# One fp32 matmul per sample on four column tiles for the Gram products of a recommendation network

## The chip, the cores and the metric

The kernel runs on one core of one Trainium2 chip. The metric is the device time of one execution in microseconds (us). A core has five engines that work side by side and meet at semaphores: TensorE (PE, with its weight loads shown apart as PEld), VectorE (DVE), ScalarE (ACT), GpSimd (POOL) and SyncE (SP), which here issues all DMA transfers. TensorE writes to PSUM (8 banks of 128 partitions x 512 fp32 values); everything else lives in SBUF.

## The reference

2048 samples, each a 27 x 128 matrix x. Each sample's Gram matrix x x^T gives 351 pair products (below the diagonal), which together with the sample's first row feed five dense layers (480 to 1024, 1024, 512, 256 and 1 outputs).

```python
bottom_mlp_output = bottom_output[:, 0, :]
interaction = jnp.einsum('bnd,bmd->bnm', bottom_output, bottom_output)
interaction_flat = interaction[:, _TRIL_R, _TRIL_C]
x = jnp.concatenate([bottom_mlp_output, interaction_flat, zero_pad], axis=1)
x = jax.nn.relu(x @ W0.T + b0)
x = jax.nn.relu(x @ W1.T + b1)
x = jax.nn.relu(x @ W2.T + b2)
x = jax.nn.relu(x @ W3.T + b3)
return x @ W4.T + b4
```

All is float32.

## The kernel before

**Chunks and layers.** The samples are worked on in 4 chunks of 512 (CHUNK). The dense layers hold the features in partitions and the samples in columns, and each fp32 product is split in two parts of a reduced type (fp32r): hi is the rounded value, lo the rest, and `product` (L1115) adds three matmuls, lo x hi, hi x hi and hi x lo (L1117 to L1119), in one PSUM bank. Two banks (`work`) take turns for the tiles of layers 0 and 1; four (`acc`) collect layers 2 to 4; two (`gps`) hold the Grams and the transposed pairs. The last chunk's layer 1 runs in another form (`layers_last`) that has no part in this. ScalarE applies the relu, VectorE splits its output into hi and lo.

**Slices.** The inputs come in slices of 32 samples (SLICE_GROUPS = 8 groups of GROUP = 4 samples), 16 slices a chunk: 128 partitions (the 128 values of an input row) x 864 columns (32 samples x 27 rows), 432 KB each. Four slices make a sub-chunk of 128 samples (SUB). One chunk's Grams are made while the chunk ahead of it goes through its layers; only chunk 0's stand by themselves.

**Grams of chunks 1 to 3.** For a slice, VectorE writes xs from xraw: hi (L733), then lo (L735), each sample padded to 32 columns (`input_parts`). A Gram half (`gram_half`) is 16 samples: four matmuls (L1143), each with four samples' hi as weights (123 columns) and their hi and lo as moving columns (224). Only the four diagonal blocks of the result are of use. ScalarE takes them out of PSUM with four copies, one for each block of 32 partitions (L541). VectorE adds 0.5 x (hi hi) + (hi lo) for a slice (`half_sum`, L751); after each fourth slice it transposes 32 x 32 blocks (L793) and adds each picked block to its mirrored one (L797, `pair_products`), which gives 378 pair slots. TensorE transposes them (L1156), ScalarE and VectorE write them as hi and lo into featH and featL, the input of layer 0.

**Grams of chunk 0.** VectorE copies each slice, padded, into xpad (`pad_input`, L969). Eight plain fp32 matmuls a slice (`first_gram`, L1129) take four samples as weights (128 columns) and 108 moving columns into two banks. ScalarE takes out four blocks a slice (L557), VectorE transposes and picks (`first_pairs`, L782 and L786). Then `layer0_left` computes the first 256 samples' layer 0, after which the first Gram half of chunk 1 and two tiles of the rest run. Before them VectorE clears the padding of xs (`zero_pads`, L963), for which TensorE waits (L1355, L1374).

**Order.** Each engine's order is written by hand. `plans` names the steps (one product of a dense layer each) after which a Gram half and a transposition stand: in chunks 1 to 3's making one half about every third step, with `interleave` doing the same for ScalarE and VectorE. xraw has XSLOTS = 4 slots, xfirst (chunk 0 only) 8 more. SyncE issues x, w0, w1, w2 and w3 in one queue (`load_x`, `load_w1`, `keep_w1`, `refill_w1`): a slot of xraw is filled again when its lo part is made, xs when the Grams four slices back are done.

Of the kernel before, what the change touches and what calls it, by code (L numbers as in the profile page):

```python
# [18 lines left out]
EVEN = INPUTS + INPUTS % 2  # L19
GCOLS = GROUP * EVEN  # L20
USED = (GROUP - 1) * QUAD + INPUTS
# [19 lines left out]
XSLOTS = 4  # L41
FIRST_SLOTS = 2 * XSLOTS
# [44 lines left out]
def rec_program(nc, x_t, x0_t, w0, w1, w2, w3, w4, biases, b4, out):  # L87
# [5 lines left out]
    with ctx:  # L93
# [19 lines left out]
        with nc.sbuf_tensor("xfirst", [P, FIRST_SLOTS, SCOLS], f32) as xfirst:  # L113
            pass
# [19 lines left out]
        xraw = sb("xraw", [P, XSLOTS, SCOLS])  # L134
        x0raw = sb("x0raw", [P, CHUNK])
        grams2 = sb("grams2", [P, 2, SLICE_GROUPS, 2, INPUTS])
# [10 lines left out]
        with nc.sbuf_tensor("xpad", [P, 2 * XSLOTS, SLICE_GROUPS * GROUP, QUAD], f32) as xpad:  # L147
            pass

        xs = sb("xs", [P, XSLOTS, 2, SLICE_GROUPS * GROUP, QUAD], f32r)  # L150

# [16 lines left out]
        x_first = [sem(f"x_first{i}") for i in range(XSLOTS + FIRST_SLOTS)]  # L168
# [3 lines left out]
        xpads_zero, pads_done = sem("xpads_zero"), sem("pads_done")  # L172
# [7 lines left out]
        xpad_done = sem("xpad_done")  # L180
        xh_done, xl_done = sem("xh_done"), sem("xl_done")
        gram_done, grams_out, half_sums = sem("gram_done"), sem("grams_out"), sem("half_sums")
# [24 lines left out]
        def by_sample(buf, p):  # L207
            return buf[:, p % XSLOTS, :].rearrange("p (b n) -> p b n", n=INPUTS)

        def first_slot(p):  # L210

            if XSLOTS <= p < XSLOTS + FIRST_SLOTS:
                return xfirst[:, p - XSLOTS, :]
            return xraw[:, p % XSLOTS, :]

        def loads_of_slot(g, p):

            return SLICES // XSLOTS * (g - 1) + 1 + p // XSLOTS + 1
# [40 lines left out]

        def parts(g, p):  # L260

            return SLICES * (g - 1) + p + 1
# [66 lines left out]
        AHEAD = XSLOTS - 1  # L329

        def loads_at(m):

            return range(2 * m + 2 * XSLOTS + 2, min(2 * m + 2 * XSLOTS + 4, SLICES))
# [4 lines left out]
        def first_banks(p):  # L338

            banks = gps[:, :, :], acc[:, 0:2, :], work[:, :, :]  # L340
            return banks[p % 3]

        def banks_used(p):

            return p - 3

        def first_grams(s):

            return grams2[:, :, :, :, :].rearrange("p a g t n -> p (a g t) n") if s % 2 else grams[:, :, :]
# [38 lines left out]
        def _(sp):  # L388
            def load_x(g, p):
                n = SLICES * g + p  # L390
                if n < XSLOTS + FIRST_SLOTS:
                    sp.dma_start(first_slot(p), x_t[n, :, :]).then_inc(x_first[p], 16)
                    return
                if n < SLICES:
                    sp.wait_ge(xpad_done, n - XSLOTS - FIRST_SLOTS + 1)
                elif n < SLICES + XSLOTS:
                    sp.wait_ge(xpad_done, n - XSLOTS + 1)
                elif p < XSLOTS:
                    sp.wait_ge(gram_done, 2 * (n - XSLOTS + 1))
                else:  # L400
                    sp.wait_ge(xl_done, parts(g, p - XSLOTS))
                sp.dma_start(xraw[:, p % XSLOTS, :], x_t[n, :, :]).then_inc(x_in[p % XSLOTS], 16)
# [68 lines left out]
            def body(c):  # L471
# [3 lines left out]
                if c == 0:  # L475
                    x_before_keep = {0: (4, 5), 1: (6, 7, 8), 2: (9, 10), 3: (11, 12), 4: (13, 14), 5: (15,)}
                elif more:
                    for p in range(XSLOTS, 2 * XSLOTS + 2):
                        load_x(c + 1, p)
# [49 lines left out]
        def _(act):  # L529
            def grams_from_psum(g, h):  # L530

                n = HALVES * g + h
                act.wait_ge(gram_done, n + 1)
                if h % 2 == 0 and h >= 4:
                    act.wait_ge(half_sums, SLICES * (g - 1) + h // 2 - 1)
                at = h % 2 * HALF_GROUPS
                for q in range(GROUP):
                    rows = slice(q * QUAD, min((q + 1) * QUAD, USED))
                    src = gps[rows].rearrange("p b (g w) -> p (b g) w", w=2 * P)[:, :, 0:2 * GCOLS]
                    src = src.rearrange("p g (t c) -> p g t c", c=GCOLS)  # L540
                    last = act.activation(grams2[rows, h // 2 % 2, at:at + HALF_GROUPS, :, :],  # L541
                                          src[:, :, :, q * EVEN:q * EVEN + INPUTS], ACT.Copy)
                last.then_inc(grams_out, 1)

            def first_from_psum(p):
# [6 lines left out]
                for q in range(GROUP):  # L552
                    rows = slice(q * QUAD, (q + 1) * QUAD)
                    src = first_banks(p)[rows, :, 0:HALF_GROUPS * GROUP * INPUTS]
                    src = src.rearrange("p b (g c) -> p b g c", c=GROUP * INPUTS)
                    dst = first_grams(s)[rows, at:at + SLICE_GROUPS, :].rearrange("p (b g) n -> p b g n", b=2)
                    last = act.activation(dst, src[:, :, :, q * INPUTS:(q + 1) * INPUTS], ACT.Copy)  # L557
                last.then_inc(grams_out, 2)
# [165 lines left out]
        def _(dve):  # L724
            for i in range(XSLOTS):
                dve.memset(xpad[:, 2 * i:2 * i + 2, :, INPUTS:], 0.0).then_inc(xpads_zero, 1)

            def input_parts(g, p):
                n = SLICES * g + p
                hi, lo = xs[:, p % XSLOTS, 0, :, 0:INPUTS], xs[:, p % XSLOTS, 1, :, 0:INPUTS]  # L730
                dve.wait_ge(x_in[p % XSLOTS], 16 * loads_of_slot(g, p))
                ge(dve, gram_done, 2 * (n - XSLOTS + 1))
                dve.tensor_copy(hi, by_sample(xraw, p)).then_inc(xh_done, 1)  # L733
                dve.wait_ge(xh_done, parts(g, p))
                dve.tensor_tensor(lo, by_sample(xraw, p), hi.bitcast(f32), ALU.subtract).then_inc(xl_done, 1)  # L735
# [8 lines left out]

            def half_sum(g, p):

                n = SLICES * g + p
                dve.wait_ge(grams_out, 2 * (n + 1))
                ge(dve, turned_done, SUBS * g + p // SLICES_SUB)
                at = p % SLICES_SUB * SLICE_GROUPS  # L750
                dve.scalar_tensor_tensor(out=grams[0:USED, at:at + SLICE_GROUPS, :],  # L751
                                         in0=grams2[0:USED, p % 2, :, 0, :], scalar=0.5,
                                         in1=grams2[0:USED, p % 2, :, 1, :], op0=ALU.mult, op1=ALU.add)\
                   .then_inc(half_sums, 1)

            def rectangles():
# [3 lines left out]
                def both(at, col, blocks, apart, rows, cols):  # L760
# [4 lines left out]
                    across = bass.AP(v.tensor, v.offset + col * QUAD,  # L765
                                     [v.ap[0], (apart * DIAG, blocks), (1, rows), (QUAD, cols)])
                    return dst, direct, across
# [10 lines left out]
            def first_pairs(s):  # L778

                dve.wait_ge(grams_out, 2 * SLICES_SUB * (s + 1))  # L780
                ge(dve, pairs_done, PAIR_OPS * s)
                dve.transpose(turned[:, :, :], first_grams(s).rearrange("p g m -> p m g")).then_inc(turned_done, 1)  # L782
                dve.wait_ge(turned_done, s + 1)
                ge(dve, pairs_t, s)
                for dst, one, _ in rectangles():
                    dve.tensor_copy(dst, one).then_inc(pairs_done, 1)  # L786

            def pair_products(g, s):

                n = SUBS * g + s  # L790
                dve.wait_ge(half_sums, SLICES_SUB * (n + 1 - SUBS))
                dve.wait_ge(pairs_done, PAIR_OPS * n)
                dve.transpose(turned[:, :, :], grams[:, :, :].rearrange("p g m -> p m g")).then_inc(turned_done, 1)  # L793
                dve.wait_ge(turned_done, n + 1)
                dve.wait_ge(pairs_t, n)
                for dst, one, other in rectangles():
                    dve.tensor_tensor(dst, one, other, ALU.add).then_inc(pairs_done, 1)  # L797

            def half_point(g, h):

                p = h // 2
                if h % 2 == 0:
                    ahead = AHEAD if g > 1 else AHEAD - 1
                    if p + ahead < SLICES:
                        input_parts(g, p + ahead)
                else:
                    half_sum(g, p)
                    if p % SLICES_SUB == SLICES_SUB - 1:
                        pair_products(g, p // SLICES_SUB)
# [151 lines left out]
            def zero_pads(i):  # L961
# [480 lines left out]
```

## Time and profile before

| | us |
|---|---|
| median of the runs (3) | 476.79 |
| lowest and highest | 475.68, 477.36 |
| the profiled execution | 477.05 |
| its span, first to last instruction | 475.3 |
| TensorE, VectorE, ScalarE busy in it | 464.9, 321.1, 264.6 |

The profiled execution's own time is 1.75 us over its span, which is what lies around the program. Its mean granted TensorE clock is 0.996 of full speed (1.00 is 2.4 GHz). A busy time is the sum of an engine's instructions; on TensorE, whose matmuls overlap, the distance from one start to the next is the better measure. An fp32 matmul of the program stands in the trace as two records of weight load and two of matmul, an fp32r one as one of each.

### The profile page before, as it was taken

Reading aid. Unit: us, or ns where it says so; the run is one execution under the profiler, and the core shown is the slowest. Engines: PE = TensorE matmul, PEld = TensorE weight load, DVE = VectorE, ACT = ScalarE, POOL = GpSimd, SP = SyncE. Lnnn points to the kernel's source line nnn. Section 1 sums busy time; section 2 is a strip of 40 time slices with the busy share of each in tenths; the row PEclk is TensorE's granted clock in tenths of the full one; section 3 lists DMA queues with packets and bytes.
Section 4 is the critical chain, followed back from the end, with each engine's and each line's share of the span. In section 5 each row is a group of like instructions: output and inputs, shape, how many; then the busy total and the mean of one; then the engine's idle time right before and its main releaser. Section 6 shows DMA issues by size and latency. Waiting matters only on the chain.

```text
span 475.3 us, 7112 instructions
## 1 busy us (share of the span) xinstructions
PE 464.9 (98%) x2599; PEld 397.1 (84%) x2599; DVE 321.1 (68%) x570; ACT 264.6 (56%) x615; POOL 0.7 (0%) x6
## 2 busy tenths in 40 slices
PE   8999899999999999999999999999999999999996
PEld 8998888888888788888888878888888778899983
DVE  4698679796849878574616877765725988766244
ACT  3896477677664377555563366565553556233241
POOL 0000000000000000000000000000000000000000
PEclk9999899999999999999999999999999999999999
DMA  8998626856225630743345243653234420460100
GB/s 301 383 341 292 207 76 207 299 192 226 92 90 201 263 106 23 308 164 116 131 159 210 56 132 125 238 215 125 90 94 170 137 89 0 134 214 11 44 1 0
DMA packets 24226, 74.40 MB, mean 157 GB/s; under 512 B 3072, under 2 KB 9216, under 8 KB 20608
## 3 DMA queue, kind: packets, MB, share of 16 engines
q1 hardware_dynamic: 24192, 73.95, 44.1%
q8 instruction: 21, 0.34, 0.3%
q14 instruction: 13, 0.11, 0.1%
HBM read 65.55 MB, written 8.40 MB: 156 GB/s over the span
## 4 chain that ended last, share of the span: by engine, by line
PE 87%; DVE 7%; ACT 4%; issue 2%; POOLq 0%; POOL 0%; DVEq 0%
PE work L1117 16%; PE work L1119 15%; PE work L1118 15%; PE gps L1143 9%; PE acc L1117 8%; PE acc L1119 7%; PE acc L1118 7%; ACT grams L557 2%; PE gps L1129 1%; PE gps L1119 1%; PE gps L1118 1%; PE gps L1117 1%; PE work L1129 1%; PE acc L1129 1%; ACT w0h L592 1%
## 5 line engine op out<-in xcount | busy, mean ns | idle before, releaser
L541 ACT ACTIVATE grams<-gps 32x216 f32<-32x216 f32 (+1 forms) x384 | 131.4, 342 | 86.5 <-PE gps L1143 83.0
L1117 PE MATMUL work<-h1h,w1s 128*128 128x512 f32 (+1 forms) x208 | 81.1, 390 | 0.0
L1119 PE MATMUL work<-h1l,w1s 128*128 128x512 f32 (+1 forms) x208 | 80.2, 386 | 0.0
L1118 PE MATMUL work<-h1h,w1s 128*128 128x512 f32 (+1 forms) x208 | 79.3, 381 | 0.0
L1143 PEld LDWEIGHTS gps<-xs 128*123 128x123 f32 x384 | 55.3, 186 | 9.7 <-issue 2.1
L1117 PE MATMUL work<-featH,w0l 126*128 126x512 f32 (+5 forms) x160 | 57.2, 358 | 3.3 <-DVE xs L963 2.1
L1143 PE MATMUL gps<-xs 128*123 128x224 f32 x384 | 57.7, 272 | 0.0
L1118 PE MATMUL work<-featH,w0h 126*128 126x512 f32 (+5 forms) x160 | 56.3, 352 | 0.0
L751 DVE SCALAR_TENSOR_TENSOR grams<-grams 123x216 f32<-123x216 f32 x48 | 18.4, 383 | 56.2 <-ACT grams L541 56.2
L1119 PE MATMUL work<-featL,w0h 126*128 126x512 f32 (+5 forms) x160 | 56.0, 350 | 0.0
L735 DVE TENSOR_TENSOR xs<-xraw,xs 128x864 fp32r<-128x864 f32 x48 | 50.8, 1059 | 1.7
L1117 PE MATMUL acc<-h2h,w2l 128*128 128x512 f32 x128 | 51.0, 399 | 0.3 <-DVE w2l L954 0.3
L576 ACT ACTIVATE act_out<-work,bias 128x512 f32<-128x512 f32 (+1 forms) x56 | 36.7, 658 | 25.6 <-PE work L1119 24.3
L1119 PE MATMUL acc<-h2l,w2h 128*128 128x512 f32 x128 | 50.3, 393 | 0.0
L1118 PE MATMUL acc<-h2h,w2h 128*128 128x512 f32 x128 | 49.9, 390 | 0.0
L1119 PEld LDWEIGHTS work<-h1l,w1s 128*128 128x128 f32 x208 | 39.1, 188 | 8.3
L1117 PEld LDWEIGHTS work<-h1h,w1s 128*128 128x128 f32 x208 | 39.3, 189 | 5.6 <-DVE w1s L949 0.4
L1118 PEld LDWEIGHTS work<-h1h,w1s 128*128 128x128 f32 x208 | 39.4, 190 | 5.4
L829 DVE TENSOR_TENSOR h2l<-act_out,h2h 128x512 fp32r<-128x512 f32 x40 | 27.7, 693 | 14.7 <-ACT act_out L637 13.6
L1117 PEld LDWEIGHTS work<-featH,w0l 126*128 126x128 f32 (+2 forms) x160 | 30.8, 193 | 8.0 <-DVE xs L963 2.3
L1119 PEld LDWEIGHTS work<-featL,w0h 126*128 126x128 f32 (+2 forms) x160 | 30.8, 192 | 4.0
L1118 PEld LDWEIGHTS work<-featH,w0h 126*128 126x128 f32 (+2 forms) x160 | 31.0, 194 | 3.3
(124 smaller groups left out, 699.3 us busy)
## 6 DMA issues: line engine op xcount, KB each, us to landing
xraw<-x_t SPq DMA_DIRECT2D x56, 432.0 KB, 4.7
w1s<-w_parts SPq DMA_DIRECT2D x20, 1024.0 KB, 4.8
stage<-w_t SPq DMA_DIRECT2D x16, 512.0 KB, 5.7
w_parts<-w1s SPq DMA_DIRECT2D x8, 1024.0 KB, 4.9
xfirst<-x_t SPq DMA_DIRECT2D x8, 432.0 KB, 8.5
w0raw<-w_t SPq DMA_DIRECT2D x4, 512.0 KB, 9.5
w2raw<-w_t SPq DMA_DIRECT2D x4, 512.0 KB, 6.6
h1l<-w_parts SPq DMA_DIRECT2D x8, 256.0 KB, 4.0
```

The costliest lines, as they stand in the source:

```text
L541: last = act.activation(grams2[rows, h // 2 % 2, at:at + HALF_GROUPS, :, :], src[:, :, :, q * EVEN:q * EVEN + INPUTS], ACT.Copy)
L557: last = act.activation(dst, src[:, :, :, q * INPUTS:(q + 1) * INPUTS], ACT.Copy)
L576: act.activation(act_out[:, slot(layer, m, more), cols], bank[:, cols], ACT.Relu, bias=bias[:, row:row + 1]).then_inc(relu_done, 1)
L592: act.activation(w0_piece(w0h, n), w0_piece(w0raw, n), ACT.Copy).then_inc(w0_hi, 1)
L735: dve.tensor_tensor(lo, by_sample(xraw, p), hi.bitcast(f32), ALU.subtract).then_inc(xl_done, 1)
L751: dve.scalar_tensor_tensor(out=grams[0:USED, at:at + SLICE_GROUPS, :], in0=grams2[0:USED, p % 2, :, 0, :], scalar=0.5, in1=grams2[0:USED, ...
L829: dve.tensor_tensor(lo, full, hi.bitcast(f32), ALU.subtract).then_inc(split_done, 1)
L1117: pe.matmul(dst, wl, ah, start=start, stop=False)
L1118: pe.matmul(dst, wh, ah, start=False, stop=False)
L1119: return pe.matmul(dst, wh, al, start=False, stop=stop)
L1129: last = pe.matmul(first_banks(p)[:, k // HALF_GROUPS, at:at + GROUP * INPUTS], four.rearrange("p b n -> p (b n)"), four[:, :, 0:INPUTS], ...
L1143: last = pe.matmul(gps[0:USED, j // 2, j % 2 * 2 * P:j % 2 * 2 * P + 2 * GCOLS], xs[:, p % XSLOTS, 0, four, :].rearrange("p b n -> p (b n) ...
```

## The change

All Grams, of every chunk, are made in one way: each sample by a plain fp32 matmul of its own, with the sample's 27 columns of the landed slice both as weights and as moving columns. Sample q of each four goes to column tile q (`tile_position=(0, 32 q)`), so that its 27 x 27 result lies in partitions 32 q to 32 q + 26, in columns of its own group.

- No padded or split copy of the input: `input_parts`, `pad_input`, `zero_pads`, xs and xpad are gone, and so is `half_sum`. VectorE clears six banks once at the start.
- One copy out of PSUM for a half (128 x 108) or, in chunk 0, for a slice (128 x 216), where there were four. A half now takes one bank and the halves alternate, so TensorE waits for the copy before the last one (`grams_out`, n - 1).
- `pair_picks` copies one block of each mirrored pair in all chunks, where chunks 1 to 3 added the two.
- xraw has 8 slots, xfirst 8; chunk 0's 16 slices are loaded without a wait. Later loads wait for the Gram that last read the slot, and their places in SyncE's queue are moved.
- Chunk 0 uses six banks in turn, and its transpositions, w0's hi parts and VectorE's steps stand in a new order.

```diff
-XSLOTS = 4
-FIRST_SLOTS = 2 * XSLOTS
+XSLOTS = 8
...
-        W0_HI_AFTER = [8, 10, 12, 14]
+        W0_HI_AFTER = [10, 12, 14, 15]
-        TRANSPOSE_AT = SLICES_SUB + 2
+        TRANSPOSE_AT = SLICES_SUB + 3
...
+                sp.wait_ge(gram_done, 2 * ((p if g == 1 and p < XSLOTS else n - XSLOTS) + 1))
                 sp.dma_start(xraw[:, p % XSLOTS, :], x_t[n, :, :]).then_inc(x_in[p % XSLOTS], 16)
...
-                    x_before_keep = {0: (4, 5), 1: (6, 7, 8), 2: (9, 10), 3: (11, 12), 4: (13, 14), 5: (15,)}
+                    x_before_keep = {0: (8,), 1: (9,), 2: (10, 11), 3: (12, 13), 4: (14,), 5: (15,)}
...
-                for q in range(GROUP):
-                    rows = slice(q * QUAD, min((q + 1) * QUAD, USED))
...
+                act.activation(sub_grams(sub)[:, at:at + HALF_GROUPS, :],
+                               gps[:, h % 2, 0:HALF_COLS].rearrange("p (g n) -> p g n", n=INPUTS), ACT.Copy)\
+                   .then_inc(grams_out, 1)
...
+            def grams_of(bank, samples, groups):
+
+                for j, k in enumerate(groups):
+                    for q in range(GROUP):
+                        one = samples[:, (k * GROUP + q) * INPUTS:(k * GROUP + q + 1) * INPUTS]
+                        last = pe.matmul(bank[q * QUAD:q * QUAD + INPUTS, j * INPUTS:(j + 1) * INPUTS], one, one,
+                                         start=True, stop=True, tile_position=(0, q * QUAD))
+                return last
...
             def gram_half(g, h, turned_before):
 
                 n, p = HALVES * g + h, h // 2
-                pe.wait_ge(xl_done, parts(g, p))
-                pe.wait_ge(grams_out, n)
+                if h % 2 == 0:
+                    pe.wait_ge(x_in[p % XSLOTS], 16 * loads_of_slot(g, p))
+                pe.wait_ge(grams_out, n - 1)
                 if g > 1 or turned_before:
                     pe.wait_ge(pairs_lo, SUBS * g + turned_before)
-                for j in range(HALF_GROUPS):
-                    k = h % 2 * HALF_GROUPS + j
-                    four = slice(k * GROUP, (k + 1) * GROUP)
-                    last = pe.matmul(gps[0:USED, j // 2, j % 2 * 2 * P:j % 2 * 2 * P + 2 * GCOLS],
-                                     xs[:, p % XSLOTS, 0, four, :].rearrange("p b n -> p (b n)")[:, 0:USED],
-                                     xs[:, p % XSLOTS, :, four, 0:EVEN], start=True, stop=True)
-                last.then_inc(gram_done, 1)
+                groups = range(h % 2 * HALF_GROUPS, (h % 2 + 1) * HALF_GROUPS)
+                grams_of(gps[:, h % 2, :], xraw[:, p % XSLOTS, :], groups).then_inc(gram_done, 1)
```

How TensorE's order changes, first in chunk 1's layer 0 while chunk 2's Grams are made. A row is line, operation, output<-inputs (the names of the program's tiles), size and how many stand in a row. Before:

```order
L1119 MATMUL work<-featL,w0h 128x512
L1143 MATMUL gps<-xs 123x224 x4
L1117 MATMUL work<-featH,w0l 128x512
L1118 MATMUL work<-featH,w0h 128x512
L1119 MATMUL work<-featL,w0h 128x512
```

After:

```order
L1013 MATMUL work<-featL,w0h 128x512
L1020 MATMUL gps<-xraw 27x27 x16
L1011 MATMUL work<-featH,w0l 128x512
L1012 MATMUL work<-featH,w0h 128x512
L1013 MATMUL work<-featL,w0h 128x512
```

The half stands at the same place; its 4 wide matmuls have become 16 narrow ones.

TensorE at the start of chunk 0, behind the warm-up's 15 transpositions. Before:

```order
L1346 MATMUL acc<-ident 128x128 x15
L1129 MATMUL gps<-xpad 128x108 x8
L1129 MATMUL acc<-xpad 128x108 x8
L1129 MATMUL work<-xpad 128x108 x8
L1129 MATMUL gps<-xpad 128x108 x8
```

After (x64 are two slices, of 32 matmuls each, in a tensor's two banks):

```order
L1242 MATMUL acc<-ident 128x128 x15
L1020 MATMUL gps<-xraw 27x27 x64
L1020 MATMUL acc<-xraw 27x27 x64
L1020 MATMUL work<-xraw 27x27 x64
L1020 MATMUL gps<-xraw 27x27 x64
```

A slice has 32 matmuls instead of 8, reads the landed data itself, and takes one bank instead of two.

## Rows read from the trace of the kernel before

**Rows 1.** The page's head and its first table: busy us, share, instructions per engine.

```profile
span 475.3 us, 7112 instructions
PE 464.9 (98%) x2599; PEld 397.1 (84%) x2599; DVE 321.1 (68%) x570; ACT 264.6 (56%) x615; POOL 0.7 (0%) x6
```

**Rows 2.** Busy time by stretch (start:end, length, each engine, granted clock, DMA share, GB/s).

```profile
core 0: us, PE busy (x) PEld busy (x) DVE busy (x) ACT busy (x) POOL busy (x), PEclk, DMA share, GB/s
5.00:36.00 31.00, 30.71 (x266) 30.39 (x265) 21.52 (x40) 24.58 (x67) 0.00 (x0) 1.00 0.98 365
...
49.00:54.00 5.00, 3.58 (x31) 3.38 (x29) 4.83 (x11) 2.68 (x7) 0.00 (x0) 1.00 0.81 265
54.00:57.00 3.00, 2.31 (x11) 2.31 (x12) 1.82 (x6) 0.00 (x0) 0.00 (x0) 0.62 0.95 327
57.00:60.00 3.00, 3.00 (x23) 3.00 (x23) 0.63 (x2) 1.84 (x5) 0.00 (x0) 0.81 0.12 50
...
75.00:390.00 315.00, 314.65 (x1564) 259.41 (x1563) 217.72 (x372) 185.32 (x446) 0.00 (x0) 1.00 0.45 158
390.00:475.30 85.30, 80.21 (x503) 70.25 (x501) 48.40 (x88) 29.99 (x44) 0.00 (x0) 1.00 0.18 56
```

**Rows 3.** The chain in order of time (start, us, what), in chunk 1's layers.

```profile
195.08 0.23 PE acc L1119
195.32 0.43 PE gps L1143 x4
195.75 0.23 PE acc L1117
...
197.59 0.23 PE acc L1119
197.82 0.43 PE gps L1143 x4
```

**Rows 4.** Groups by line and shape: xcount, busy us, mean ns, idle before.

```profile
L541 ACT ACTIVATE grams<-gps 32x216 f32<-32x216 f32 x288 | 98.4, 342 | 85.4 <-PE gps L1143 83.0
...
L1143 PE MATMUL gps<-xs 128*123 128x224 f32 x384 | 57.7, 272 | 0.0
...
L735 DVE TENSOR_TENSOR xs<-xraw,xs 128x864 fp32r<-128x864 f32 x48 | 50.8, 1059 | 1.7
...
L733 DVE CAST xs<-xraw 128x864 fp32r<-128x864 f32 x48 | 28.9, 603 | 0.0
...
L751 DVE SCALAR_TENSOR_TENSOR grams<-grams 123x216 f32<-123x216 f32 x48 | 18.4, 383 | 56.2 <-ACT grams L541 56.2
...
L1129 PEld LDWEIGHTS acc<-xpad 128*128 128x128 f32 x80 | 9.3, 192 | 0.0
...
L1118 PE MATMUL gps<-th,sh 128*128 128x256 f32 x32 | 9.1, 283 | 0.0
```

**Rows 5.** The chain in order of time, chunk 0's Grams.

```profile
4.97 2.78 PE gps L1129 x16
7.75 1.79 PE acc L1129 x16
...
20.57 1.80 PE work L1129 x16
22.74 0.34 ACT grams L557
```

**Rows 6.** Waits of TensorE, 0 to 75 us: who, for whom, us, times, longest.

```profile
PE work L1117 <- DVE xs L963: 2.1, 1, 2.1
...
PE work L1117 <- ACT act_out L576: 0.6, 1, 0.6
PE work L1117 <- ACT act_out L587: 0.4, 2, 0.2
```

**Rows 7.** Timeline of VectorE and TensorE at 52 to 55 us (start, us, instruction).

```profile
51.92 0.60 DVE L733 CAST xs<-xraw 128x864 fp32r<-128x864 f32 x1
52.56 1.06 DVE L735 TENSOR_TENSOR xs<-xraw,xs 128x864 fp32r<-128x864 f32 x1
53.63 1.00 DVE L963 MEMSET xs<- 128x320 f32 x3
...
54.69 0.58 PE L1117 MATMUL work<-featH,w0l 128*128 128x256 f32 x1 [2.10 <-DVE xs L963]
```

**Rows 8.** DMA issues: count, KB each, median us to landing.

```profile
xraw<-x_t SPq DMA_DIRECT2D x56, 432.0 KB, 4.7
w1s<-w_parts SPq DMA_DIRECT2D x20, 1024.0 KB, 4.8
...
w0raw<-w_t SPq DMA_DIRECT2D x4, 512.0 KB, 9.5
...
x0raw<-x_t SPq DMA_DIRECT2D x4, 256.0 KB, 6.7
```

**Rows 9.** One tile's instructions (ns min/median/max) and the chain; first w4s, xs, then chain.

```profile
L1339 PEld LDWEIGHTS acc<-h2h,w4s x8: 82/82/83, 163.0 to 470.6; 128*1 128x1 f32 x8
...
L1143 PEld LDWEIGHTS gps<-xs x384: 182/184/330, 49.0 to 358.4; 128*123 128x123 f32 x192
...
162.96 0.23 PE work L1119
163.19 0.24 PE acc L1338
...
164.36 0.23 PE acc L1341
164.59 0.23 PE work L1117
```

**Rows 10.** Timeline of TensorE, the last slice of chunk 0.

```profile
33.66 2.04 PE L1129 MATMUL gps<-xpad 128*128 128x108 f32 x16
```

More of the change, by code:

```diff
@@ L167, in rec_program @@
         x_in = [sem(f"x_in{i}") for i in range(XSLOTS)]
-        x_first = [sem(f"x_first{i}") for i in range(XSLOTS + FIRST_SLOTS)]
+        x_first = [sem(f"x_first{i}") for i in range(SLICES)]
         x0_in = sem("x0_in")
@@ L475, in body @@
                 if c == 0:
-                    x_before_keep = {0: (4, 5), 1: (6, 7, 8), 2: (9, 10), 3: (11, 12), 4: (13, 14), 5: (15,)}
+                    x_before_keep = {0: (8,), 1: (9,), 2: (10, 11), 3: (12, 13), 4: (14,), 5: (15,)}
                 elif more:
-                    for p in range(XSLOTS, 2 * XSLOTS + 2):
+                    for p in range(XSLOTS, XSLOTS + 4):
                         load_x(c + 1, p)
@@ L551, in first_from_psum @@
                 at = p % SLICES_SUB * SLICE_GROUPS
[L552 to L558, printed above, removed]
+                act.activation(sub_grams(s)[:, at:at + SLICE_GROUPS, :],
+                               first_bank(p).rearrange("p (g n) -> p g n", n=INPUTS), ACT.Copy).then_inc(grams_out, 2)
             def pairs_hi_part(g, s, first=False):
@@ L724, in _ @@
         def _(dve):
[L725 to L735, printed above, removed]
+            for p in range(FIRST_BANKS):
+                dve.memset(first_bank(p), 0.0).then_inc(banks_zero, 1)
             def dense_parts(g):
@@ L764, in both @@
                                      [v.ap[0], (apart * DIAG, blocks), (QUAD, rows), (1, cols)])
-                    across = bass.AP(v.tensor, v.offset + col * QUAD,
-                                     [v.ap[0], (apart * DIAG, blocks), (1, rows), (QUAD, cols)])
-                    return dst, direct, across
+                    return dst, direct
                 at = 0
@@ L776, in rectangles, with pair_picks @@
                 yield both(at, INPUTS - ENDS, 1, 0, INPUTS, ENDS)
[L778 to L785, printed above, removed]
-                    dve.tensor_copy(dst, one).then_inc(pairs_done, 1)
[L788 to L797, printed above, removed]
-            def half_point(g, h):
[L801 to L809, printed above, removed]
+            def pair_picks(g, s):
+                n = SUBS * g + s
+                dve.wait_ge(grams_out, 2 * SLICES_SUB * (n + 1))
+                ge(dve, pairs_done, PAIR_OPS * n)
+                dve.transpose(turned[:, :, :], sub_grams(s).rearrange("p g m -> p m g")).then_inc(turned_done, 1)
+                dve.wait_ge(turned_done, n + 1)
+                ge(dve, pairs_t, n)
+                for dst, one in rectangles():
+                    dve.tensor_copy(dst, one).then_inc(pairs_done, 1)
+            def half_point(g, h):
+                if h % (2 * SLICES_SUB) == 2 * SLICES_SUB - 1:
+                    pair_picks(g, h // (2 * SLICES_SUB))
             def pairs_lo_part(g, s, first=False):
@@ L1012, in _ @@
             half_point(1, 0)
-            for i in range(1, XSLOTS):
-                zero_pads(i)
             def body(c, more):
@@ L1091, in body @@
                         s_lo_part(0, 1)
-                if later:
-                    input_parts(c + 2, 1)
                 if c + 1 == LAST:
```

133 lines of the change are left out of this document (34 added, 99 removed).

## The prediction

> **What bounds the kernel now.** I read the page's first table for the engine that is full, then the table of stretches for where it is full, then the chain for what a Gram costs there, then the groups by shape for the price of one instruction. [rows 1]: TensorE is busy for 464.9 of 475.3 us, VectorE for 321.1, ScalarE for 264.6. The stretches say where that share is real [rows 2]: from 75 to 390 us TensorE is idle for 315.00 - 314.65 = 0.35 us. The idle time lies at 49 to 57 us (1.4 + 0.7 us) and behind 390 us, where no Gram is computed. So in chunks 1 to 3 every ns that a Gram half takes on TensorE is in the time, and no ns that ScalarE or VectorE saves there is.
>
> The chain confirms it [rows 3]: between the big matmuls, one every 0.23 us, stands a Gram half, L1143 x4, of 0.43 us. There are 384 / 4 = 96 of them [rows 4], 41.3 us, 8.6% of the span in the chain's shares. In chunk 0 a slice takes 16 records, 1.79 us [rows 5]; from 22.4 us on the chain passes to ScalarE, whose four evictions take 0.34 us each. An fp32 matmul stands there as two records of weight load and matmul: 8 matmuls a slice, 16 records. An fp32r one is a single record.
>
> **What the change removes off the path.** VectorE loses the hi and lo parts (603 + 1059 ns) and the half sum (383 ns) of 48 slices, 98 us; ScalarE loses three of four evictions of 342 ns, 96 halves, so about 98 us, and the one left is narrower (108 columns, not 216) [rows 4]. In chunks 1 to 3 this runs beside a TensorE that is never idle: 0 us. Three places of the early stage are different:
> - VectorE's pads and the input parts ahead of them hold TensorE for 2.1 us at 52.6 us [rows 6, 7]. Both are gone. What is late next is a relu, for which TensorE waits 0.6 and 0.4 us in this stretch already [rows 6]. Gain 2 us.
> - Behind that gap the clock is 0.62 for 3 us and 0.81 for 3 us [rows 2]: 1.1 + 0.6 = 1.7 us lost to the lower level. Without the gap I give back 1 us of it.
> - In chunk 0 ScalarE leaves the chain, but TensorE's own 16 slices remain: 2.78 + 15 x 1.79 us [rows 5]. Removing the pad copies brings little, since the first slice waits for the warm-up too. With the cost found below it comes to 15 x (1.79 - 1.73) = 1 us.
>
> Together -4 us. The eight slots and direct loads hide nothing that is waited for: behind 75 us no TensorE wait of weight is a DMA's [rows 2]. The SyncE queue does get a new wait, on the Gram itself, with the w1 transfers queued behind it; the loads run eight slices, some 16 x 2.5 = 40 us, ahead of their use, so I cost it at 0. If that cover failed, layer 1 would wait for w1s and lose a landing, 4.8 us [rows 8]. The new order of VectorE and ScalarE in chunk 0 (picks one slice later) also costs 0 while TensorE's slices are the slower ones.
>
> **What it adds on the path.** Half a slice is 16 samples: 16 fp32 matmuls of 27x27, so 32 records of weight load and matmul, where there were 4. The whole sum is the price r of one record.
> - Weight load. It is 82 ns for one column, 184 for 123, 192 for 128 [rows 4, 5, 9]: (184 - 82) / 122 and (192 - 82) / 127 give 0.84 to 0.87 ns a column, and the rest is latency. The spacing agrees: 0.43 / 4 = 107.5 ns for 123 columns, 1.79 / 16 = 111.9 for 128. Take off 96 columns x 0.85 and 27 columns are 107.5 - 82 = 26 ns.
> - Matmul. 108 moving columns fit in 111.9 ns with their load; 27 then need at most 28 ns.
> - Load and matmul overlap today (224 columns are 93 ns at 2.4 GHz, 123 of weights 0.85 x 123 = 105, the pair 107.5), so they needn't be added.
>
> With no use of the other three tiles r = 26 to 28; I take **27 ns**. The half is 32 x 27 = 0.86 us, +0.43 us against 0.43; 96 halves: **+41.7 us**. In chunk 0 a slice is 64 x 27 = 1.73 us, counted above.
>
> The bounds lie far apart, since no row shows a narrow weight load beside a narrow matmul. From below: four tiles that work fully side by side, 27 / 4 = 7 ns. From above: a record costs what today's does whatever its width, 107.5 to 112 ns. I take 27 because both slopes lead to it, and because each record still is a load and a matmul of one instruction stream. Its densest stretch today is two instructions in 107.5 ns, and that is set by the load's width, so it is no floor of issue.
>
> Weighed against a page. The 1-column weights of layer 4 stand between 128-column ones, and the step into them and out of them is 0.23 to 0.24 us, the same as without [rows 9]. So I charge nothing for a change of shape; whether these ran on a small tile the row doesn't say. The Trainium skill, TensorEngine Tiling (Array Packing), section Tiling Modes, says that changing the tiling mode (not just the tile) drains TensorE. By that rule, with a matmul's latency of 283 - 107 = 176 ns (256 columns, [rows 4]) exposed twice in each half, the sum would be 96 x 0.35 = 34 us more.
>
> **Sum.** Against the profiled execution's own 477.05 us (span 475.3 and 1.75 around it): 477.05 + 41.7 - 4 = 514.8; its distance to the median of the runs shown, 476.79, is -0.26: **514.5 us**.
>
> **Rivals.**
> 1. *The tiles overlap.* Four column tiles write four PSUM quadrants and share nothing but the rows; with loads and matmuls side by side r is 7 to 14 ns. The half is 0.22 to 0.45 us, so 96 halves give -20 to +2 us. Chunk 0 would then run at the pace of its data: 16 slices of 0.442 MB, four pieces of w0 and x0 are 9.4 MB [rows 8], at 365 GB/s [rows 2] 26 us from 2 us on, so 28 us where the last slice's Grams now end at 33.66 + 2.04 = 35.7 [rows 10]: -8 us; with -3 of the other places, **445 to 467 us**. For it: each tile has its own weights and outputs, and a wait only for its own. Against: a weight load has never been seen beside another here. The point from which it decides: 96 x (32 r - 0.43) = 8 us of gain elsewhere, r = 16 ns. The Trainium skill, TensorE: Matmul & The Clock Gate, Part 3, has matmuls on different tiles starting about 4 ns apart, which is this rival's rule; the same page's section "Wait — 56ns, not 53.3ns?" says that starts never come closer than about 25 ns however narrow the matmul, by which (an estimate) the half is 0.8 us and the time 508. No row here has matmuls narrow enough to show either.
> 2. *A floor of issue.* Two instructions per record go through one sequencer. If a record can't cost less than 40 to 54 ns (half of today's densest pair), a half is 1.28 to 1.72 us: +82 to +124 us; chunk 0 pays 16 x (64 r - 1.79) = +12 to +27 us. With -3: **568 to 625 us**. For it: 4096 new records, 8192 instructions, are more than the 7112 in the whole trace [rows 1]. Against: nothing but the absence of a row.
> 3. *Width saves nothing* (r = 107.5 to 112): +290 to +303 us and +81 to +86 in chunk 0, **about 850 us**. Against it: the load does get shorter with fewer columns [rows 9].
> 4. *The clock.* TensorE's stream in chunk 0 becomes one of narrow work; after the idle time at 52.6 us the granted clock was 0.62 to 0.81 [rows 2], part of it at the 1.2 GHz level. If chunk 0 ran at that level its 27.7 us of Grams would double: 514.5 + 28 = **542 us**. Against: today's narrow 108-column matmuls hold 1.00.
> 5. *The tile argument doesn't do what it says*, all samples in one place after another: that is the forecast's own price, and the same time.
>
> **How the numbers follow.** Forecast 0.42 (r from 20 to 38 ns, 490 to 560 us), overlap 0.25, floor of issue 0.25, clock 0.05, width saves nothing 0.03. A measurement of this kernel tells about 0.3% from no change, 1.4 us. Faster is rival 1 nearly alone: 0.25. Same is a narrow band around r = 16: 0.02. Slower 0.73. The range from 443 to 625 us takes in the overlap's best and the floor's 54 ns; rival 3 and a part of the floor lie above it. The forecast's own range is 490 to 560 us.
>
> **What would show it.** Spacing of the new records in the chain: 0.86 us per half (32 records) in chunks 1 to 3 for the forecast, under 0.5 for rival 1, over 1.2 for rival 2; the pace between halves otherwise still 0.23 us per big matmul; 1.7 us a slice in chunk 0. TensorE still without idle time from 75 to 390 us plus what is added; VectorE's busy sum down by about 100 us and ScalarE's by more than 98; the 2.1 us wait at 52 us gone. The prediction is wrong if r isn't 20 to 38 ns, if a drain shows at the step into a half, or if TensorE is seen to wait in chunks 1 to 3 for a slice or for w1.

## The result

The changed kernel takes 494.85 us (median of 4 runs, 494.37 to 495.4), the kernel before 476.97: a ratio of 1.038, with a 95% interval of 1.0357 to 1.0404. The profiled execution's span is 492.7 us, 17.4 more than before's 475.3. The forecast was 514.5 us, in a range of 443 to 625: slower was right, but less than half of the forecast loss came, and it lies in other places.

The page's head, its first table, the granted clock in 40 slices (9 stands for 90% or more) and the queue that fetches instructions (packets, MB, share of 16 DMA engines):

```profile
span 492.7 us, 13402 instructions
...
PE 458.7 (93%) x6055; PEld 363.6 (74%) x6055; DVE 214.8 (44%) x408; ACT 140.3 (28%) x279; POOL 0.7 (0%) x6
...
PEclk9555899999999999999999999999999999999999
...
q8 instruction: 48, 0.79, 0.7%
```

and the last of these in the kernel before:

```profile
q8 instruction: 21, 0.34, 0.3%
```

VectorE lost 106 us of work and ScalarE 124, as the change means them to; TensorE has 2.3 times the records of [rows 1], and its clock is at the lower level (0.5, which is 1.2 GHz) from about 12 to 49 us. The instruction packets are of 16 KB (0.79 MB / 48). Taking a load and a matmul as one instruction each, TensorE has 12110 of them, 47.3 x 256, and 48 packets; before it had 5198, 20.3 x 256, and 21 packets. So one packet carries 256 of TensorE's instructions, a block in what follows. Busy time by stretch, as in [rows 2]:

```profile
core 0: us, PE busy (x) PEld busy (x) DVE busy (x) ACT busy (x) POOL busy (x), PEclk, DMA share, GB/s
...
5.00:36.00 31.00, 10.70 (x714) 9.47 (x715) 7.73 (x16) 5.30 (x13) 0.00 (x0) 0.60 1.02 388
36.00:49.00 13.00, 5.79 (x319) 5.09 (x319) 5.34 (x9) 4.20 (x9) 0.00 (x0) 0.50 0.77 305
49.00:60.00 11.00, 11.00 (x83) 11.00 (x82) 8.02 (x20) 5.57 (x12) 0.00 (x0) 0.87 0.01 2
...
75.00:130.00 55.00, 55.00 (x842) 41.07 (x841) 25.55 (x42) 16.91 (x36) 0.00 (x0) 1.00 0.57 201
```

From 5 to 36 us TensorE works for 10.70 us where it worked for 30.71. Its timeline has the first matmul of layer 0 at 49.04 us, where the one before has

```profile
35.99 0.39 PE L1117 MATMUL work<-featH,w0l 128*128 128x256 f32 x1 [0.29 <-ACT grams L557]
```

The chain in order of time shows what stands in between in the changed kernel (start, us, what; some of its pieces are left out):

```profile
7.73 0.31 PE acc L1020 x14
8.03 3.75 issue
11.78 0.81 PE acc L1020 x47
12.59 0.90 PE work L1020 x77
13.49 5.58 issue
19.07 0.81 PE work L1020 x50
19.93 0.85 PE gps L1020 x73
20.78 4.48 issue
```

Bursts of some 128 records (47 + 77 and 50 + 73 have pieces of their own), 256 instructions, take 1.7 us (2.7 with three transpositions among them), and between them stand 2.3 to 5.6 us of "issue": TensorE waits for nothing that the program asked it to wait for. There are seven such pieces, 27.4 us in all. From 5 to 49 us the instruction queue has eight packets. While the DMA engines are full one burst starts 6.0 to 7.3 us after the other (11.78, 19.07 and so on to 43.63 us).

From 75 us until the last Gram TensorE is never idle, and the chain in a layer with its Gram half, to be read against [rows 3], is

```profile
206.55 0.23 PE acc L1013
206.77 0.35 PE gps L1020 x32
207.12 0.43 PE acc L1011
207.55 0.23 PE acc L1012
```

32 records cost 0.35 us, less than the 0.43 us of the four wide ones; but the matmul behind them takes 0.43 us, where any other takes 0.23. So from half to half it is 2.62 us (206.77 to 209.39 in the same view), where it was 2.50 us [rows 3].

**The account of the span.** Chunk 0 +13.0 us (49.04 - 35.99); 96 halves x 0.11 = +10.6 us (from chunk 1's second half to the last one, 94 steps, it is 308.7 us against 298.5, 0.109 a step); so the rest, 17.4 - 23.6 = -6.2 us, was gained in the early layers, where before had its 2.1 us wait and its lowered clock [rows 2, 6].

### The profile page after: what moved, and what is told of

The parts are those of the page before. It is cut to its first block, busy times and chain, and to the rows that moved or that the text cites. A ratio compares the mean times of both kernels' runs of the same rounds, so it can differ in the third digit from the quotient of the medians.

```text
span 492.7 us, 13402 instructions
## 1 busy us (share of the span) xinstructions
PE 458.7 (93%) x6055; PEld 363.6 (74%) x6055; DVE 214.8 (44%) x408; ACT 140.3 (28%) x279; POOL 0.7 (0%) x6
## 4 chain that ended last, share of the span: by engine, by line
PE 89%; issue 6%; DVE 3%; DMA 1%; ACT 0%; SPq 0%; DVEq 0%
PE work L1011 19%; PE work L1012 16%; PE work L1013 16%; PE acc L1011 8%; PE gps L1020 8%; PE acc L1013 7%; PE acc L1012 7%; PE gps L1013 1%; PE gps L1012 1%; PE gps L1011 1%; DMA xraw<-x_t 1%; PE acc L1020 1%; PE gps L1052 1%; DVE h1l L755 1%; PE work L1020 1%
## 5 line engine op out<-in xcount | busy, mean ns | idle before, releaser
L1011 PE MATMUL work<-h1h,w1s 128*128 128x512 f32 (+1 forms) x208 | 86.6, 416 | 0.0
L1012 PE MATMUL work<-h1h,w1s 128*128 128x512 f32 (+1 forms) x208 | 79.8, 384 | 0.0
L511 ACT ACTIVATE grams<-gps 128x108 f32<-128x108 f32 x96 | 25.1, 261 | 160.9 <-PE gps L1020 160.9
L1020 PEld LDWEIGHTS gps<-xraw 128*27 128x27 f32 x3328 | 33.5, 107 | 37.8 <-issue 37.0
L1011 PE MATMUL work<-featH,w0l 126*128 126x512 f32 (+5 forms) x160 | 59.2, 370 | 0.0
L753 DVE CAST h2h<-act_out 128x512 fp32r<-128x512 f32 x32 | 13.6, 425 | 96.2 <-ACT act_out L541 96.2
L1011 PE MATMUL acc<-h2h,w2l 128*128 128x512 f32 x128 | 52.6, 411 | 0.0
L1020 PE MATMUL gps<-xraw 128*27 128x27 f32 x3328 | 44.1, 193 | 4.5 <-issue 4.5
L726 DVE STREAM_TRANSPOSE turned<-grams 128x864 f32<-128x864 f32 x16 | 30.7, 1916 | 34.6 <-ACT grams L511 24.8
L755 DVE TENSOR_TENSOR h2l<-act_out,h2h 128x512 fp32r<-128x512 f32 x40 | 27.7, 692 | 14.7 <-ACT act_out L602 13.6
L1012 PEld LDWEIGHTS work<-featH,w0h 126*128 126x128 f32 (+2 forms) x160 | 31.1, 194 | 3.3
## 6 DMA issues: line engine op xcount, KB each, us to landing
w2raw<-w_t SPq DMA_DIRECT2D x4, 512.0 KB, 13.8
```

Of the source, the lines that this page charges most:

```text
L511: act.activation(sub_grams(sub)[:, at:at + HALF_GROUPS, :], gps[:, h % 2, 0:HALF_COLS].rearrange("p (g n) -> p g n", n=INPUTS), ACT.Copy)\
L726: dve.transpose(turned[:, :, :], sub_grams(s).rearrange("p g m -> p m g")).then_inc(turned_done, 1)
L753: dve.tensor_copy(hi, full).then_inc(hi_done, 1)
L755: dve.tensor_tensor(lo, full, hi.bitcast(f32), ALU.subtract).then_inc(split_done, 1)
L1011: pe.matmul(dst, wl, ah, start=start, stop=False)
L1012: pe.matmul(dst, wh, ah, start=False, stop=False)
```

## The experiments

My theory after the result: two losses that have nothing to do with each other. In chunk 0 a run of narrow matmuls uses up instructions faster than they are fetched, and the fetches queue behind the data. In chunks 1 to 3 the tiles do overlap, some 7 ns a record, but each burst (the narrow matmuls that stand together) pays a fixed price of about 0.3 us. The rivals stand in the expectations.

### One part of the change alone: e1_wide0

Chunk 0 of the kernel before, chunks 1 to 3 of the changed one, with 4 slots of xraw. In the kernel before:

```diff
 def gram_half(g, h, turned_before):
     n, p = HALVES * g + h, h // 2
-    pe.wait_ge(xl_done, parts(g, p))
-    pe.wait_ge(grams_out, n)
+    if h % 2 == 0:
+        pe.wait_ge(x_in[p % XSLOTS], 16 * loads_of_slot(g, p))
+    pe.wait_ge(grams_out, n - 1)
...
+    groups = range(h % 2 * HALF_GROUPS, (h % 2 + 1) * HALF_GROUPS)
+    grams_of(gps[:, h % 2, :], xraw[:, p % XSLOTS, :], groups, 0).then_inc(gram_done, 1)
```

> Chunk 0 stays as in the kernel before (xpad, wide fp32 matmuls, 4 slots of xraw); only the Grams of chunks 1 to 3 are made per sample on four column tiles from the landed slice, without xs, hi, lo and half sum. Theory A (two separate losses: 13 us in chunk 0, and 0.11 to 0.12 us in each of 96 halves): chunk 0 as before, +11 us from the halves, -3 us from the pads gone, so 484 to 486 us. Rival (chunk 0's form costs nothing by itself, the halves and the slots carry the loss): 492 to 495 us, as the changed kernel.

Measured: 480.92 us, against 476.08 of before on the same chip, a ratio of 1.0107 (1.0077 to 1.0137). So chunk 0's form, with the eight slots and the places of the loads that go with it, costs 494.85 - 480.92 = 13.9 us; in it layer 0 starts at 35.53 us, 13.5 earlier than in the changed kernel. The gain of the early layers was under-estimated here too: layer 2's first matmul starts at 76.8 us, before's at 81.5. 480.92 lies 3 us below what I expected, mostly for that reason.

### Chunk 0: who holds the instructions back

e3_quiet, the changed kernel with one wait in SyncE's queue:

```diff
+            sp.wait_ge(gram_done, HALVES)
             for p in range(2):
                 load_x(1, p)
             for m in range(2):
                 load_w1(m)
```

> The changed kernel; SyncE issues nothing behind chunk 0's slices, w0 and x0 until all of chunk 0's Grams are done. Theory A (TensorE's instruction fetch starves behind the data transfers): the gaps of 3 to 5.6 us between bursts of some 127 records stay while slices and w0 land, up to about 27 us, and are under 2 us after it; layer 0 starts at 36 to 43 us instead of 49.4; total 484 to 491 us, if the later arrival of w1 and w2 costs little. Rival B (the sequencer itself can't issue more than a record in some 50 ns on a long run of narrow matmuls): gaps unchanged, layer 0 at 49 us, total 494 us or more.

Measured: 487.92 us, 1.0248 (1.0222 to 1.0274) of before, 6.9 us less than the changed kernel (6.4 by the spans of the profiled executions). Its chain in chunk 0, first while the slices and w0 land and then (from 28 us on) as the transfers run out:

```profile
8.36 3.69 issue
...
13.76 5.88 issue
...
21.34 4.50 issue
...
28.52 2.14 issue
...
32.38 2.03 issue
...
37.08 0.84 issue
...
39.63 1.70 issue
```

The first three gaps stay (14.1 us in all, 13.8 in the changed kernel), with the DMA engines at 1.00 (8.3 to 26 us); the last four, with these at 0.02 to 0.04 (from 28.5 us on), come to 6.7 us instead of 13.6. Layer 0 starts at 42.78 us, 6.3 us earlier. The expectation of theory A held, but for two gaps just above its 2 us.

e14_alone goes further: no Gram starts until all 16 slices have landed, and w0 and all later loads wait for the Grams.

```diff
+            sp.wait_ge(gram_done, HALVES)
+            for n in range(W0_LOADS):
...
                 pe.wait_ge(x_first[p], 16)
+                if p == 0:
+                    for n in range(SLICES):
+                        pe.wait_ge(x_first[n], 16)
+                    pe.wait_ge(x0_in, 16)
```

> The changed kernel, with chunk 0's Grams starting only when all 16 slices have landed, and w0 and all later loads held until the Grams are done: no data transfer runs beside them. What it costs as a whole (some 20 us for waiting) is not the question. Theory A (the gaps are instruction fetches that queue behind data): gaps of 0.8 to 2 us instead of 3.3 to 5.9, 128 records in 2.5 to 3.7 us instead of 6.2; all 8 blocks in 20 to 30 us. Rival B (a pace of TensorE's sequencer): 128 records in 6.2 us as before.

Measured: 505.5 us as a whole. Two stretches of it and pieces of its chain:

```profile
26.00:34.00 8.00, 3.30 (x273) 2.94 (x263) 2.50 (x6) 1.68 (x5) 0.00 (x0) 0.77 0.02 4
34.00:44.00 10.00, 5.20 (x315) 4.56 (x314) 4.05 (x9) 1.97 (x6) 0.00 (x0) 0.50 0.01 3
```

```profile
26.23 1.81 issue
...
29.40 2.59 issue
...
38.67 1.06 issue
```

With 0.01 to 0.02 of the DMA engines busy the gaps are 1.1 to 2.6 us, 12.6 in all, and a burst starts 3.4 to 4.0 us after the other instead of 6.0 to 7.3. So rival B, a pace of the sequencer that makes 6.2 us whatever is transferred, falls: the same instructions come faster when nothing is transferred. But even then the Grams of chunk 0 take from 23.6 to 51.9 us, 28.3 us, and that is what 16 wide slices of 1.79 us take (28.6 us). My bound of 0.8 to 2 us was somewhat low.

e9_halves asks how the fetch shares a DMA engine with the data:

```diff
-                    sp.dma_start(first_slot(p), x_t[n, :, :]).then_inc(x_first[p], 16)
+                    for at in range(0, SCOLS, SCOLS // 2):
+                        sp.dma_start(first_slot(p)[:, at:at + SCOLS // 2], x_t[n, :, at:at + SCOLS // 2])\
+                          .then_inc(x_first[p], 16)
...
-                pe.wait_ge(x_first[p], 16)
+                pe.wait_ge(x_first[p], 32)
```

> The changed kernel with each of chunk 0's slices loaded by two DMAs of 432 columns (1728 bytes a row instead of 3456), the same bytes. Theory A1 (an instruction fetch takes turns with the data's rows on a DMA engine, so it waits in proportion to their size): gaps of 4.5 us while the slices land fall to 2.5 to 3 us. Rival A2 (it shares bandwidth, or waits for the queue as such): gaps unchanged at 3.7 to 5.9 us, total 494 us.

Measured: 495.47 us (one execution), gaps of 3.1 to 4.5 us, 26.2 us in all, where the changed kernel has 27.4. Neither expectation is met. The four gaps while the halved slices land (3.34, 3.12, 3.94, 3.51) come to 13.9 us against 17.3 in the changed kernel, a fifth less and not the two fifths of A1; the three behind them, beside transfers of the old form, to 12.3 against 10.0. That the instructions come later while data is transferred is shown; by what rule they wait is open.

### Chunks 1 to 3: the price of a record

e8_onetile, all 16 samples of a half on one tile:

```diff
-                grams_of(gps[:, h % 2, :], xraw[:, p % XSLOTS, :], groups).then_inc(gram_done, 1)
...
+                        at = (j * GROUP + q) * INPUTS
+                        last = pe.matmul(gps[0:INPUTS, h % 2, at:at + INPUTS], one, one,
+                                         start=True, stop=True, tile_position=(0, 0))
+                last.then_inc(gram_done, 1)
```

> The changed kernel, but in chunks 1 to 3 all 16 samples of a half go to column tile 0, side by side in the bank's columns, so that ScalarE's copy no longer holds all the results. Theory A (the low price of a record comes from four tiles that work side by side): a record costs 20 to 30 ns, a half 0.3 us + 32 x 26 ns = 1.1 us, +0.6 us a half: 540 to 570 us. Rival (a narrow load and matmul cost 7 to 11 ns on any tile): no change, 494 us.

Measured: 555.37 us (one execution). TensorE's timeline around a half in it (start, us, and the records merged in one row):

```profile
206.22 1.06 PE L1046 MATMUL gps<-xraw 128*27 128x27 f32 x32
207.21 0.50 PE L1011 MATMUL work<-featH,w0l 126*128 126x512 f32 x1
207.55 0.40 PE L1012 MATMUL work<-featH,w0h 126*128 126x512 f32 x1
```

and in the changed kernel:

```profile
206.70 0.42 PE L1020 MATMUL gps<-xraw 128*27 128x27 f32 x32
207.06 0.50 PE L1011 MATMUL acc<-h2h,w2l 128*128 128x512 f32 x1
```

One record's own duration is 188 ns; 32 on one tile take 1.06 us, so they start (1.06 - 0.188) / 31 = 28 ns apart; on four tiles (0.42 - 0.188) / 31 = 7.5 ns. The four tiles work side by side, load and matmul both.

The Trainium skill, TensorE: Matmul & The Clock Gate, Part 3, has starts of about 4 ns on different tiles (here it is 7.5, with a weight load to each matmul), and its section "Wait — 56ns, not 53.3ns?" a floor of about 25 ns: the second fits what one tile shows (28 ns), and it isn't one across tiles (7.5 ns).

e4_eight leaves out half of the samples of each half:

```diff
-                groups = range(h % 2 * HALF_GROUPS, (h % 2 + 1) * HALF_GROUPS)
+                groups = range(h % 2 * HALF_GROUPS, (h % 2 + 1) * HALF_GROUPS - 2)
```

> The changed kernel with half of the samples left out of each Gram half in chunks 1 to 3: 8 matmuls (16 records) instead of 16 (32). Theory A (a half costs some 7.5 ns a record and 0.3 us fixed for going into and out of the narrow shape): 16 x 7.5 = 0.12 us less a half, 96 halves, 11.5 us less: about 483 us. Rival (no fixed part, 0.54 / 32 = 17 ns a record): 26 us less, 469 us.

Measured: 484.54 us (one execution), 10.3 us less. Its chain:

```profile
207.57 0.24 PE gps L1020 x16
207.81 0.43 PE work L1011
```

Each of the 16 records left out takes (0.35 - 0.24) / 16 = 7 ns off, and the 0.43 us of the next matmul stays. So the rest is fixed: 0.24 - 16 x 0.007 = 0.13 us ahead and 0.43 - 0.23 = 0.20 us behind.

### Where the fixed price comes from

e11_wide_fp32, plain fp32 on the whole array, four samples a matmul (only part of the results is copied out):

```diff
-                grams_of(gps[:, h % 2, :], xraw[:, p % XSLOTS, :], groups).then_inc(gram_done, 1)
...
+                    four = xraw[:, p % XSLOTS, k * GROUP * INPUTS:(k + 1) * GROUP * INPUTS]
+                    last = pe.matmul(gps[0:GROUP * INPUTS, h % 2, j * GROUP * INPUTS:(j + 1) * GROUP * INPUTS], four, four,
+                                     start=True, stop=True)
```

> The changed kernel, but in chunks 1 to 3 a half is 4 plain fp32 matmuls of four samples each (108 weight columns, 108 moving, 8 records) on the whole array; what is copied out is then only part of the results. It asks where the fixed price of 0.3 us comes from. Theory A (going from the whole array to column tiles and back drains TensorE): no fixed price, a half is 8 x 95 ns = 0.76 us and the next product is 0.23 us again: +0.2 us a half against 0.78 - 0.23 = 0.55: 510 to 516 us. Rival (the step between fp32r and plain fp32 is what costs): the fixed price stays, a half is 0.76 + 0.3 us, 540 us.

e12_narrow_r, the kernel before with narrow weights in its fp32r matmuls:

```diff
-                    last = pe.matmul(gps[0:USED, j // 2, j % 2 * 2 * P:j % 2 * 2 * P + 2 * GCOLS],
-                                     xs[:, p % XSLOTS, 0, four, :].rearrange("p b n -> p (b n)")[:, 0:USED],
+                    last = pe.matmul(gps[0:INPUTS, j // 2, j % 2 * 2 * P:j % 2 * 2 * P + 2 * GCOLS],
+                                     xs[:, p % XSLOTS, 0, four, :].rearrange("p b n -> p (b n)")[:, 0:INPUTS],
```

> The kernel before, with the 4 matmuls of each half in chunks 1 to 3 given only one sample's 27 columns as weights instead of four samples' 123 (fp32r, 224 moving columns, output on 27 partitions, which puts them on a tile of 128x32); three quarters of the Grams are left out by it. It asks whether the fixed price comes with the narrow tile alone, as layer 4's one-column weights didn't show it. Theory A (any step between the whole array and a column tile costs it): the half's own time is 4 x 97 ns = 0.39 us, the start is 0.08 us late and the next product 0.43 us instead of 0.23: 0.2 us a half more than before, 490 us or more. Rival (only plain fp32 on a narrow tile pays it): the next product is 0.23 us, and the time is 473 to 476 us.

Measured: 516.54 us and 474.28 us (one execution each). The chain of e11_wide_fp32:

```profile
205.94 0.76 PE gps L1044 x8
206.70 0.25 PE work L1011
```

and of e12_narrow_r:

```profile
207.55 0.42 PE gps L1144 x4
207.97 0.24 PE work L1118
```

Neither pays. Plain fp32 on the whole array doesn't, and fp32r on a narrow tile doesn't; plain fp32 on a narrow tile does, on one tile (the 0.43 us behind it in e8_onetile) as on four. That e12's matmuls are on a narrow tile isn't read from the trace, which shows no tile: in the built program they are marked 128 x 32, like the Grams of the changed kernel and like layer 4's one-column matmuls, and all others 128 x 128. Each expectation was right about one half of it: the theory for e11 (its 510 to 516 us just missed), the rival for e12.

The Trainium skill's rule (TensorEngine Tiling (Array Packing), Tiling Modes) that every change of the tiling mode drains TensorE is not borne out for fp32r, by e12 or by layer 4's weights [rows 9]. For plain fp32 the trace looks like it. The weight loads at the step into a burst, in the changed kernel and then in e12_narrow_r:

```profile
206.16 0.19 PEld L1013 LDWEIGHTS acc<-h2l,w2h 128*128 128x128 f32 x1
206.70 0.31 PEld L1020 LDWEIGHTS gps<-xraw 128*27 128x27 f32 x32 [0.35 <-issue]
```

```profile
206.93 0.19 PEld L1120 LDWEIGHTS work<-h1l,w1s 128*128 128x128 f32 x1
207.16 0.55 PEld L1144 LDWEIGHTS gps<-xs 128*27 128x27 f32 x4
```

In e12 the narrow load starts at once, beside the wide matmul ahead of it (207.15 us); in the changed kernel the loads stand idle for 0.35 us first, and the narrow one starts 0.31 us after the wide matmul ahead (206.39 us). Why narrow and plain fp32 together cost this, 0.33 us in all, is open.

### A better kernel: longer bursts, a wide chunk 0

If a burst has a fixed price, fewer and longer bursts are cheaper. On e1_wide0, e5_slice makes a whole slice at every second half point (one copy of 128x216), e6_two two slices at every fourth; e13_mixed one slice at once in chunk 1 and two in chunks 2 and 3. In the form of e13_mixed (`many` slices at once):

```diff
+                if h % (2 * many) != 2 * many - 1:
+                    return
...
+                for n, at in enumerate(range(p - many + 1, p + 1)):
+                    pe.wait_ge(x_in[at % XSLOTS], 16 * loads_of_slot(g, at))
+                    last = grams_of(gps[:, p // many % 2, :], xraw[:, at % XSLOTS, :], range(SLICE_GROUPS),
+                                    n * SLICE_GROUPS)
+                last.then_inc(gram_done, 2 * many)
```

> As e1_wide0 (chunk 0 wide, chunks 1 to 3 on four column tiles), but the 32 samples of a slice go in one burst of 64 records at every second half point, with one copy of 128x216. Theory A (a burst has a fixed price of some 0.3 us and 7 to 7.5 ns a record): 48 of 96 fixed prices fall away, 14 us less than e1_wide0: 466 to 469 us. Rival (a burst of 128 instructions outruns the instruction fetch or the queue of TensorE, a gap takes the place of the fixed price): 476 to 481 us.

> As e5_slice, with two slices (64 samples, 128 records, 256 instructions) in one burst at every fourth half point, with one copy of 128x432. Theory A: 24 fixed prices fewer again, 7 us less than e5_slice: 459 to 462 us. Rival (256 instructions in about 1 us need more than one 16 KB fetch of instructions in that time, so that gaps of about 1 us show inside or behind the burst): 24 x 1 us more, 470 to 485 us.

> As e6_two, but chunk 1's Grams go slice by slice (as in e5_slice), chunks 2 and 3 two slices at once. In e6_two the gaps of 2.0 and 1.1 us inside bursts stand in chunk 1, while many loads are under way. Theory A: those 3.1 us go and 8 fixed prices of 0.3 us (2.7 us) come back: 463 to 465 us, the same as e6_two (464.7) within 0.3%. Rival (the gaps come from the bursts of two slices anywhere and were there by chance): 466 to 467 us.

| kernel | us | ratio to before, 95% interval |
|---|---|---|
| e5_slice | 468.19 | 0.9832 (0.9804 to 0.9861) |
| e6_two | 464.66 | 0.9753 (0.9721 to 0.9785) |
| e13_mixed | 463.04 | 0.9728 (0.9692 to 0.9764) |

All three beat both kernels, and e5_slice (466 to 469 us) and e13_mixed (463 to 465) came as expected; e6_two missed its 459 to 462 us and lies below its rival's 470. In the chain of e5_slice a burst is

```profile
211.30 0.67 PE gps L1080 x51
211.96 0.43 PE work L1059
```

(64 records; some have no piece of their own), and in e6_two 1.20 us with the same 0.43 behind it. e5_slice came 12.7 us below e1_wide0, near the 14 of the fixed prices; the 32 records more take 0.67 - 0.35 = 0.32 us, 10 ns each and not 7. e6_two came 3.5 us below e5_slice where 7 were expected, and its chain in chunk 1 says why:

```profile
65.20 0.98 PE gps L1080 x70
66.19 1.96 issue
68.15 0.38 PE gps L1080 x23
```

A burst of 256 instructions met the same starvation, of 2.0 and 1.1 us in chunk 1 and 0.9 us once later. Behind the first the granted clock is 0.53 from 69.5 to 72 us and 0.82 from 72 to 75, some 1.7 us more (an estimate from these shares). In the profiled executions, where the span fell by 1.2 us (465.7 to 464.5), the two make up most of what is missing. With chunk 1 slice by slice no such wait is left among TensorE's, and the time is 463.04 us; its interval overlaps e6_two's, so the last step isn't certain by the times.

## Why the prediction was right and wrong

The measured 494.85 us lies within the forecast's own 490 to 560 us, but by luck: r isn't between 20 and 38 ns, and the step into a half costs something, which the prediction itself had named as two signs of being wrong. Errors of opposite sign met.

- **The bound.** Right: behind 75 us, as long as Grams are made, TensorE is idle for no more than 0.35 us in either kernel, and taking the work for the Grams off ScalarE and VectorE (230 us in the whole kernel) gave nothing there.
- **The price of a record.** r = 27 ns was read well from two slopes for one tile (28 ns in e8_onetile), and taken for the wrong case. The step that failed is the sentence that each record is a load and a matmul of one instruction stream: four tiles start records 7.5 ns apart. The term of +41.7 us measured +10.6 us. Rival 1's lower bound, 27 / 4 = 7 ns, was the right number, though its time, 445 to 467 us, wasn't.
- **The fixed price.** It was in the sum at 0, from [rows 9]. Those rows are of fp32r, and for fp32r they were right (e12_narrow_r); for fp32 on a narrow tile it is 0.33 us a burst, 96 times, +32 us. The records by themselves, 32 x 7 ns = 0.22 us a half against 0.43, are a gain of 20 us. The two together come near the 10.6 us measured. The 34 us for two exposed latencies a half, which the prediction named and left out of its sum, are near to that in size.
- **Chunk 0.** Forecast as a gain of 1 us, measured as +13.0 us. Rival 2 named a floor of issue, but as a price per record everywhere; what binds is the fetch of 256-instruction blocks (16 KB in the page's queues), only where they are used up faster than one in 3.4 to 4.0 us (quiet) or 6.0 to 7.3 us (DMA engines full). [rows 1 and 2] held both halves of it: 7112 instructions in 475 us, and DMA engines at 0.98 in just that stretch. I compared the new instruction count with the old and didn't divide it by the time of chunk 0.
- **The clock.** Rival 4's condition came true: the granted clock was 1.00 until the first gap, of 3.75 us at 8.03 us, and 0.50 in each burst behind it. Its price of 28 us did not. A burst of 128 records takes 1.71 us at 0.50 and 1.35 us at 1.00 (28.05 to 29.40 us in e14_alone), 0.36 us seven times, and three groups of transpositions take 0.83 instead of 0.33 us, so at most 4 us. In e14_alone the next burst starts 3.9 us later at 1.00 and 3.4 to 4.0 at 0.50, so most of it was hidden in the wait for instructions. The first 12 matmuls of layer 0 took 0.21 us each, not 0.12, 1.1 us.
- **The early stage.** The gain was 6.2 us where I had 3 (without chunk 0's own): VectorE's work for chunk 1's input stood in the chain of the kernel before from 43 us on, not only at the 2.1 us wait:

```profile
43.10 0.62 DVE xs L733
...
43.74 1.06 DVE xs L735
```

- **The slots and SyncE's queue.** Costed at 0, and no wait for a slice or for w1 shows behind chunk 0. But early loads aren't free: chunk 1's first slices, w1 and w2 are transferred in the stretch in which instructions were short, and e3_quiet, which holds them back, is 6.9 us faster. What the eight slots by themselves did wasn't tested.

Three errors with different signs: 31.1 us too much for the records and the price of a burst, 14.0 too little for chunk 0, 3.2 of gain not seen. So 37.7 us were forecast and 37.7 - 31.1 + 14.0 - 3.2 = 17.4 measured in the span.

## What to carry to other kernels

Before breaking wide matmuls into many narrow ones, count the instructions per us of the stretch, and look at how full the DMA engines are there: a run that uses 256 instructions in 1.7 us starved here, by 2.3 to 5.6 us a block while data landed and by 1.1 to 2.6 us with nothing beside it, and the trace shows it as "issue" and not as a wait. Where narrow work stands between wide work, price the step from one to the other apart from the records, and make bursts as long as buffers and instruction fetches allow. Small matmuls on different column tiles did overlap (7.5 ns against 28), so the idea was sound: with longer bursts, and chunk 0 left as it was, it gave 2.7% instead of costing 3.8%.

## What was unexpected in the hardware

- Narrow plain fp32 records (27 weight columns, 27 moving) start 7.5 ns apart on four column tiles and 28 ns apart on one.
- Going into and out of such a burst costs 0.13 and 0.20 us; fp32r on a narrow tile (0.42 us for four matmuls, then 0.24 for the next) and fp32 on the whole array (0.76 us for eight records, then 0.25) cost nothing of the kind.
- TensorE's instructions come in blocks of 256; under full DMA engines a block of narrow matmuls came every 6.0 to 7.3 us, with idle ones every 3.4 to 4.0 (e14_alone).
